# A four-layer graph network on one core: nodes without incoming edges put first, edge stages joined with the dense stages behind them

## The chip, the cores and the metric

The kernel runs on 1 core of a Trainium2 chip. Its time is the device time of one execution in microseconds, the median over several. A time without a unit is in microseconds. Engines: TensorE (PE; its weight loads are PEld), VectorE (DVE), ScalarE (ACT), GpSimd (POOL) and SyncE (SP, which only issues DMAs here).

## The reference

10000 nodes of 512 numbers and 5000 directed edges, sorted by target, go through four layers; each is followed by `x = layernorm(x + layer(x))`. Cut to what matters:

```
gin:  a = x + segment_sum(x[src], dst);  relu(a @ W1 + b1) @ W2 + b2
sage: m = segment_sum(x[src], dst) / max(count, 1)
      h = m @ W_l.T + b_l + x @ W_r.T;  relu(batch_norm(h)) + x
gat:  twice (edges and self loops, H = 4 heads of C = 256):
      h = (x @ W).reshape(n, H, C)
      e = leaky_relu(al_s[src] + al_d[dst], 0.2)        # al_s, al_d: h dotted with a_src, a_dst
      w = exp(e - segment_max(e, dst)[dst]);  alpha = w / segment_sum(w, dst)[dst]
      x = relu(segment_sum(h[src] * alpha, dst) + bias)
      then x @ Wfc + bfc
gcn:  dinv = (degree + 1) ** -0.5;  xw = x @ W.T
      h = segment_sum(dinv[row] * dinv[col] * xw[row], col) + b  # with self loops
      gelu(batch_norm(h)) + x
```

A node without an incoming edge has an empty sum: its GAT weight is 1 for itself and its GCN sum is its own row.

## The kernel before, in words

Nodes are padded to G = 20 groups of 512 (GROUP), each of S = 4 subtiles of 128 rows. Edges are T = 40 tiles of 128. The matrices are multiplied in half precision with a high and a low part: `split_product` (L316) issues three matmuls a chunk of 128 (L325, L326, L327).

The program is a list of stages (L2961). `run` (L278) gives every engine its part of a stage and then lets all five drain and meet on a semaphore, so a stage begins when the last engine is done with the one before. Inside a stage the order on an engine's queue is written out by hand. The stages are, with their place in the span: setup and the edge sum of the input; `gin_stage` (L1644); `edge_product_stage` (L1086); `sage_stage` (L1843); `norm_coefficients_stage`; `batch_norm_stage` (L2040, with the first GAT product, to `h1`); `edge_attention_stage` of `h1` (L1249); `gat_middle_stage` (L2298, to `h2`); `edge_attention_stage` of `h2`; `gat_stage` 2 (L2483, the last GAT product, to `x3`); `edge_sum_stage` of `x3` (L975); `gcn_stage` (L2738); the coefficients again; `output_stage` (L2858).

**Edge stages.** An edge stage goes over the 40 tiles. POOL gathers the source rows by an indirect DMA; a 128x128 matrix made from `apart` (which edges of the tile have different targets) sums rows with the same target on PE; SP stores the 128 sums of the tile to DRAM `sum` or `sum_gat` and, separately, its first and last row, for targets that cross from tile to tile (the rim, joined in a few steps at the end). In the attention stage a tile passes around a ring: ACT spreads the scores (L1496), PE turns them (L1543), DVE masks and takes maxima (L1380, L1385, L1387, L1391), ACT takes the exponential (L1511), PE sums the weights (L1552), DVE makes the matrix `a_lhs` of all four heads (L1397 to L1414), PE multiplies it with the gathered rows (L1560), ACT brings the result to SBUF (L1519), SP stores it. There are two buffers of `a_masked`, `a_lhs` and the score banks.

**Dense stages.** A node's sum lies in a slot that `slot_i` names, nodes without edges at a slot of zeros, so every dense stage starts with `gather_sums` (L1637): four indirect DMAs a group on POOL. In the GAT stages DVE combines own row and sums (`t_z`, L2415 and L2420, L2622), ACT applies bias and relu (L2433, L2656), makes the high part (L2436, L2659), POOL the low part (L2389, L2591). In GCN the low part is DVE's (L2798). In SAGE own rows come by one plain load a group, and PE turns both own rows (L1978) and sums. POOL adds the bias rows in GIN (L1732) and batch norm (L2161).

**Layer norm.** `Norm` (L1594): DVE takes statistics and aggregates (L1608, L1611), POOL raises variance to -1/2 (L1617, L1620), and a row operation applies it. The rows of the output stage: DVE adds residual and branch (L2923), `Norm`, POOL makes the shift `-mean * power` by two small operations (L2908, L2911), ACT applies (L2943), SP stores one group of 1 MB by one DMA (L2896):

```
sp.wait_ge(rows_out.sem, rows_out.at(g * S + S))
sp.dma_start(node_rows(dram["out"], *divmod(g, 2)), x[g])
```

## Time and profile before

| what | value |
| --- | --- |
| three runs | 3909.58, 3916.79, 3917.03; median 3916.79 |
| the profiled execution | 3912.85, its span 3911.1 |
| mean granted TensorE clock | 0.932 |
| busy PE / PEld / DVE / ACT / POOL | 3419.3 (87%) / 2074.1 (53%) / 2155.2 (55%) / 1463.1 (37%) / 1452.1 (37%) |
| DMA | 821.41 MB, mean 210 GB/s |

The stages, by the first and last instruction of each: setup and edge sum to 199.5; GIN to 659.5; edge product to 835; SAGE to 1131.5; coefficients to 1137; batch norm to 1627.5; attention of `h1` to 1812.7; GAT middle to 2687.9; attention of `h2` to 2873.5; second GAT product to 3402.1; edge sum of `x3` to 3495.6; GCN to 3758.5; coefficients to 3763.5; output to 3911.

A matmul's end is modelled, so a busy PE can still be slower than its peak. An engine's busy share over the whole span mixes stages with different limits, so the stages are read one by one.

### The profile page before, as it was taken

The page shows a single profiled execution, that of the slowest core. Times are in us where ns is not written, and L with a number is a line of the kernel's source. Part 1 is how long each engine was busy: PE and PEld are TensorE (multiplying, and loading weights), DVE is VectorE, ACT ScalarE, POOL GpSimd, SP SyncE. Part 2 cuts the span into 40 slices and gives each one's busy share as a digit, 9 for nine tenths or more (in the row PEclk, how much of TensorE's full clock was granted, in tenths as well). Part 3 has the DMA queues.
Part 4 walks back from the last instruction along what each step waited for, and adds up shares of the span by engine and source line. Part 5 has one row for each costly group of instructions (what it writes and reads, how often), then busy time and mean ns, then how long its engine had stood idle before and what let it go on. Part 6 is the DMA issues. An engine that isn't in the chain of part 4 may idle for free. (4 is left out here: it accounts for less than half of the span.)

```text
span 3911.1 us, 55988 instructions
## 1 busy us (share of the span) xinstructions
PE 3419.3 (87%) x19416; PEld 2074.1 (53%) x19416; DVE 2155.2 (55%) x3972; ACT 1463.1 (37%) x2580; POOL 1452.1 (37%) x1231
## 2 busy tenths in 40 slices
PE   4669998989969999886999999998859999859964
PEld 3234443545637666664666666666635555315543
DVE  7257775845554444276543443413758888406667
ACT  1323332533324444353332332322534444233357
POOL 2345553225422222253333323212536666343312
PEclk7789999989979999997999999999979999979976
DMA  2667774656659999597978878944957777375558
GB/s 82 201 184 198 196 201 146 201 172 228 227 195 259 279 274 281 180 280 213 256 192 204 204 194 198 200 119 146 280 209 259 262 261 262 123 231 186 174 167 275
DMA packets 624227, 821.41 MB, mean 210 GB/s; under 512 B 378374, under 2 KB 378374, under 8 KB 622032
## 3 DMA queue, kind: packets, MB, share of 16 engines
q1 hardware_dynamic: 556880, 598.37, 50.3%
q0 software_dynamic: 67200, 221.25, 20.1%
q8 instruction: 71, 1.16, 0.1%
q14 instruction: 76, 0.62, 0.1%
HBM read 470.83 MB, written 263.59 MB: 188 GB/s over the span
## 5 line engine op out<-in xcount | busy, mean ns | idle before, releaser
L326 PE MATMUL bank<-w_lo,t_r_hi 128*128 128x344 f16 (+1 forms) x2560 | 838.8, 328 | 0.0
L327 PE MATMUL bank<-w_hi,t_r_hi 128*128 128x344 f16 (+1 forms) x2560 | 838.6, 328 | 0.0
L325 PE MATMUL bank<-w_hi,w_lo 128*128 128x344 f16 (+1 forms) x2240 | 716.7, 320 | 49.8 <-DMA w_lo<-g_row_lo 31.3
L2415 DVE SCALAR_TENSOR_TENSOR t_z<-w_lo,t_z 128x256 f32<-128x256 f32 x320 | 243.5, 819 | 396.4 <-DMA w_lo<-h 393.4
L326 PE MATMUL bank<-w_lo,w_hi 128*128 128x344 f16 (+1 forms) x1280 | 419.6, 328 | 0.0
L327 PE MATMUL bank<-w_hi 128*128 128x344 f16 (+1 forms) x1280 | 419.4, 328 | 0.0
L2389 POOL TENSOR_TENSOR t_row_lo<-t_r,t_row_hi 128x1024 f16<-128x1024 f32 x80 | 174.9, 2187 | 509.8 <-ACT t_row_hi L2436 509.8
L327 PEld LDWEIGHTS bank<-w_hi,t_r_hi 128*128 128x128 f16 x2560 | 250.9, 98 | 168.8 <-issue 0.8
L326 PEld LDWEIGHTS bank<-w_lo,t_r_hi 128*128 128x128 f16 x2560 | 250.9, 98 | 162.5 <-issue 0.6
L325 PE MATMUL bank<-w_hi 128*128 128x344 f16 x960 | 298.3, 311 | 21.8 <-DMA w_hi<-t_row_lo 19.2
L325 PEld LDWEIGHTS bank<-w_hi,w_lo 128*128 128x128 f16 x2240 | 219.3, 98 | 181.7 <-issue 50.8
L325 PE MATMUL bank<-l_z_hi,w_lo 128*128 128x512 f16 x640 | 244.4, 382 | 1.4 <-DVE l_z_lo L2798 1.4
L326 PE MATMUL bank<-l_z_lo,w_hi 128*128 128x512 f16 x640 | 244.3, 382 | 0.0
L327 PE MATMUL bank<-l_z_hi,w_hi 128*128 128x512 f16 x640 | 244.1, 381 | 0.0
L325 PE MATMUL bank<-w_hi,t_r_lo 128*128 128x512 f16 x640 | 243.6, 381 | 0.0
L2591 POOL TENSOR_TENSOR t_r_lo<-t_r,t_r_hi 128x512 f16<-128x512 f32 x160 | 196.0, 1233 | 97.1 <-ACT t_r_hi L2659 90.1
L2447 ACT ACTIVATE w_hi<-bank 128x344 f32<-128x344 f32 x240 | 104.5, 454 | 339.5 <-PE bank L327 339.4
L2656 ACT ACTIVATE t_r<-bank,vec_scaled 128x512 f32<-128x512 f32 x160 | 109.6, 685 | 293.0 <-PE bank L2687 241.4
L1639 POOL DMA_INDIRECT t_z<-sum_gat,slot_i x160 | 163.0, 1019 | 122.0 <-SPq L292 79.1
L2243 ACT ACTIVATE b_wide<-bank 128x344 f32<-128x344 f32 x240 | 109.2, 456 | 253.1 <-PE bank L327 253.1
L1617 POOL TENSOR_TENSOR n_power<-n_moments,eps 128x4 f32<-128x4 f32 x80 | 15.9, 199 | 502.9 <-DVE n_moments L1611 502.9
L2622 DVE SCALAR_TENSOR_TENSOR t_z<-w_lo,t_z 128x256 f32<-128x256 f32 x320 | 187.0, 645 | 21.4 <-DMA t_z<-sum_gat,slot_i 13.3
(345 smaller groups left out, 6732.2 us busy)
## 6 DMA issues: line engine op xcount, KB each, us to landing
w_lo<-h SPq DMA_DIRECT2D x160, 512.0 KB, 5.7
h<-b_wide SPq DMA_DIRECT2D x80, 516.0 KB, 9.6
h<-w_hi SPq DMA_DIRECT2D x80, 516.0 KB, 2.9
sum_gat<-a_out SPq DMA_DIRECT2D x80, 514.0 KB
l_x<-x SPq DMA_DIRECT2D x40, 1024.0 KB, 9.1
sum<-e_out SPq DMA_DIRECT2D x120, 256.0 KB
g_x<-in_x SPq DMA_DIRECT2D x20, 1024.0 KB, 5.6
x<-g_y SPq DMA_DIRECT2D x20, 1024.0 KB, 5.1
```

Source lines behind the costliest of these rows:

```text
L325: pe.matmul(out, s_lo, m_hi, start=(k == 0), stop=False)
L326: pe.matmul(out, s_hi, m_lo, start=False, stop=False)
L327: mm = pe.matmul(out, s_hi, m_hi, start=False, stop=last)
L1617: self.nc.gpsimd.tensor_tensor(self.power[:, u, :], self.moments[:, u, :, 1], self.kn.eps[:], ALU.add)\
L1639: pool.indirect_dma_start(out, None, sums, bass.IndirectOffsetOnAxis(ap=kn.slot_i[:, g * S + s:g * S + s + 1], axis=0), bounds_check=kn.d. ...
L2243: act.activation(wide[s][:, n * THIRD:(n + 1) * THIRD], mm[n], ACT.Copy, scale=UNSCALE)\
L2389: nc.gpsimd.tensor_tensor(row_lo[:, s, :], r_f[s % 2][:], row_hi[:, s, :], ALU.subtract)\
L2415: ins = v.scalar_tensor_tensor(out=z[u][:, s, cols], in0=hrow[:, s, cols], scalar=z[u][:, s, HC + h:HC + h + 1], in1=z[u][:, s, cols], op0 ...
L2447: act.activation(wide[s % 2][:, third * THIRD:(third + 1) * THIRD], mm[s % 2][third], ACT.Copy, scale=UNSCALE).then_inc(wide_done.sem, 1)
L2591: g_.tensor_tensor(r_lo[:, u, k, :], r_f[k % 2][:], r_hi[:, u, k, :], ALU.subtract)\
L2622: ins = v.scalar_tensor_tensor(out=z[u][:, s, cols], in0=hrow[:, s, cols], scalar=z[u][:, s, HC + h:HC + h + 1], in1=z[u][:, s, cols], op0 ...
L2656: act.activation(r_f[k % 2][:], tp[k % 4][:], ACT.Relu, scale=A_SCALE, bias=kn.vec_scaled[:, bias + k:bias + k + 1]).then_inc(r_done.sem, 1)
```

## The change

After the change, "place" is a node's rank when nodes without an incoming edge come first. `d.early` = E = (10000 - 5000) // 1024 * 2 = 8 groups can't hold a node with an edge, whatever the graph.

- Setup ranks the nodes (a few operations on 128x80, three small matmuls), and keeps two tables in DRAM: `by_node` (dinv, place) and `by_place` (node, slot, dinv). GIN's POOL queue writes `by_place` by 80 small indirect stores, four behind the gathers of each group. The edge product stage reads it back, and POOL casts `slot_i` and `node_i`.
- GIN still works in node order. From SAGE on, rows lie by place: SAGE and batch norm fetch own rows of `x1` by four indirect DMAs a group on POOL (`own_rows`), where SP loaded a group at once. SAGE gathers, turns and adds sums for the last 12 groups alone. Batch norm's POOL queue also looks up place and dinv of all sources and targets (`look_up`, 80 in all, four a group).
- The two attention stages and the edge sum of `x3` are gone. The class `AttentionEdges` holds the same steps, each with one buffer of `a_masked`, `a_lhs` and scores, and the score turn as a transpose. `gat_middle_early_stage` and `rows_product_early_stage` run the first 8 groups, which need no sums, and carry 45 edge steps between their products: over 96 slots (three products a subtile) in the middle, over 32 in the second product. DVE makes the low parts in both, and `z * scale + bias` in the first; POOL only gathers for edges. `gcn_early_stage` does the same with `RowEdges`, 41 steps over 32 slots, on rows of `x3` that aren't scaled. `gat_middle_stage`, `gat_stage` and `gcn_stage` then go over 12 groups, written as before.
- The output rows lie by place: SP's plain store becomes four indirect stores a group on POOL, queued behind the next group's `Norm` and shift. DVE makes `-mean` (one operation on 128x4 a group), POOL has one small operation less.
- Small tables per edge lie in one SBUF buffer.

```diff
+        self.early = max(nodes - edges, 0) // (2 * GROUP) * 2
...
+def own_rows(kn, pool, out, g, s, landed):
+    pool.indirect_dma_start(out, None, kn.dram["x1"],
+                            bass.IndirectOffsetOnAxis(ap=kn.node_i[:, g * S + s:g * S + s + 1], axis=0),
+                            bounds_check=kn.d.padded - 1, oob_is_err=False).then_inc(landed.sem, 16)
...
+def shared_out(steps, slots):
+    return [range(n * steps // slots, (n + 1) * steps // slots) for n in range(slots)]
...
+class AttentionEdges:
+    W, O = 4, 3
...
+    def matrices(self, dve, t):
+        dve.wait_ge(self.den_done.sem, self.den_done.at(t + 1))
+        v.tensor_tensor(self.out[o][:, A_DEN], self.den_ps, self.weight[u][:, 0, :], ALU.add).then_inc(self.den_kept.sem, 1)
+        if t + 2 < self.T:
+            self.scores(dve, t + 2)
...
+        dve.wait_ge(self.summed.sem, self.summed.at(t))
+        v.scalar_tensor_tensor(out=self.lhs[:], in0=self.kn.apart[:, t, :].unsqueeze(1).broadcast_to([P, K, P]),
+                               scalar=0.0, in1=self.out[o][:, A_EDGE].unsqueeze(2).broadcast_to([P, K, P]),
+                               op0=ALU.is_equal, op1=ALU.mult).then_inc(self.lhs_ready.sem, 1)
...
+    def vector(self, dve, t):
+        self.matrices(dve, t)
+        if t + 1 < self.T:
+            self.maxima(dve, t + 1)
...
+    def steps(self):
+        return self.T + 5
...
+    def tensor(self, pe, t):
+        w = t % self.W
+        pe.wait_ge(self.lhs_ready.sem, self.lhs_ready.at(t + 1))
+        pe.wait_ge(self.evacuated.sem, self.evacuated.at(2 * t))
+        for h in range(HEADS):
+            ins = pe.matmul(self.total[h // 2][:, (h % 2) * C:(h % 2 + 1) * C], self.lhs[:, h, :],
+                            self.rows[w][:, LOGITS + h * C:LOGITS + (h + 1) * C], start=True, stop=True)
+        ins.then_inc(self.summed.sem, 1)
+        if t + 1 < self.T:
+            self.sum_weights(pe, t + 1)
+        if t + 2 < self.T:
+            self.score_rows(pe, t + 2)
...
+def gat_middle_early_stage(kn):
...
+    steps = shared_out(edges.steps(), THIRDS * N)
...
+        for j in range(N):
+            for third in range(THIRDS):
+                if j + S < N and third == 0:
+                    add_bias(j + S)
+                if j + S < N and third == 2:
+                    low_part(j + S)
+                for e in steps[j * THIRDS + third]:
+                    edges.vector_step(dve, e)
...
+            for third in range(THIRDS):
+                pe.wait_ge(wide_done.sem, wide_done.at((j - 1) * THIRDS + third + 1))
+                split_product(pe, mm[third],
+                              lambda k: (r_hi[u][:, s * CH + k, :], r_lo[u][:, s * CH + k, :]),
+                              lambda k: (kn.gat_weights(False, W_GAT2, k, third),
+                                         kn.gat_weights(True, W_GAT2, k, third)), CH).then_inc(prod.sem, 1)
+                for e in steps[j * THIRDS + third]:
+                    edges.tensor_step(pe, e)
...
+def rows_product_early_stage(kn):
...
+    steps = shared_out(edges.steps(), E * S)
...
+        low_parts(0, range(CH))
+        edges.vector_start(dve)
+        for g in range(E):
+            for s in range(S):
+                if g + 1 < E:
+                    low_parts(g + 1, (2 * s, 2 * s + 1))
+                residual(g, s)
+                for e in steps[g * S + s]:
+                    edges.vector_step(dve, e)
+                if s == 1 and g:
+                    finish(g - 1)
+        finish(E - 1)
...
+            for s in range(S):
+                if g + 1 < E:
+                    turn(g + 1, (2 * s, 2 * s + 1))
+                pe.wait_ge(y_done.sem, y_done.at(g * S + s - 1))
+                split_product(pe, mm[s % 2][:],
...
+def gcn_early_stage(kn, held):
...
+    edges = RowEdges(kn, room, dram["x3"], (kn.src_by[:, :, 0], kn.src_dinv_neg), kn.dst_dinv, kn.rim_dinv)
+    steps = shared_out(edges.steps(), 4 * E)
...
 def output_stage
-            sp.dma_start(node_rows(dram["out"], *divmod(g, 2)), x[g])\
-                .then_inc((first_stored if g < B else stored).sem, 16)
...
+        def store(g):
+            pool.wait_ge(rows_out.sem, rows_out.at(g * S + S))
+            for s in range(S):
+                pool.indirect_dma_start(dram["out"],
+                                        bass.IndirectOffsetOnAxis(ap=kn.node_i[:, g * S + s:g * S + s + 1], axis=0),
+                                        x[g][:, s, :], None, bounds_check=d.padded - 1, oob_is_err=False)\
+                    .then_inc((first_stored if g < B else stored).sem, 16)
...
-            nc.gpsimd.tensor_tensor(shift[:, u, :], norm.moments[:, u, :, 0], norm.power[:, u, :], ALU.mult)\
-                .then_inc(shifted.sem, 1)
-            pool.wait_ge(shifted.sem, shifted.at(g * 2 + 1))
-            nc.gpsimd.tensor_scalar(shift[:, u, :], shift[:, u, :], -1.0, None, ALU.mult).then_inc(shifted.sem, 1)
+            pool.wait_ge(negated.sem, negated.at(g + 1))
+            nc.gpsimd.tensor_tensor(shift[:, u, :], shift[:, u, :], norm.power[:, u, :], ALU.mult).then_inc(shifted.sem, 1)
+            if g:
+                store(g - 1)
...
+            dve.wait_ge(norm.seen.sem, norm.seen.at((g + 1) * 2 * S))
+            v.tensor_scalar(shift[:, u, :], norm.moments[:, u, :, 0], -1.0, None, ALU.mult).then_inc(negated.sem, 1)
...
-        kn.add(edge_attention_stage(kn, dram["h1"]))
+        kn.add(gat_middle_early_stage(kn))
         kn.add(gat_middle_stage(kn))
-        kn.add(edge_attention_stage(kn, dram["h2"]))
+        kn.add(rows_product_early_stage(kn))
         kn.add(gat_stage(kn, 2))
...
-            kn.add(edge_sum_stage(kn, mem, dram["x3"], (kn.src_dinv, kn.src_dinv_neg), kn.dst_dinv, kn.rim_dinv))
...
+            kn.add(gcn_early_stage(kn, held))
             kn.add(gcn_stage(kn, held))
```

## Rows read from the trace of the kernel before

**Rows 1.** Busy time by stage; us, busy (x instructions) by engine, PEclk, DMA, GB/s.

```profile
1627.50:1812.70 185.20, 143.87 (x748) 111.26 (x748) 122.94 (x462) 84.12 (x201) 79.79 (x80) 0.92 0.77 232
1812.70:2687.90 875.20, 847.35 (x5776) 567.60 (x5776) 343.81 (x402) 259.93 (x401) 254.92 (x160) 0.98 0.79 193
2687.90:2873.50 185.60, 143.40 (x748) 111.02 (x748) 122.97 (x462) 84.01 (x201) 79.66 (x80) 0.92 0.77 232
2873.50:3402.10 528.60, 489.73 (x2560) 262.61 (x2560) 388.05 (x640) 202.87 (x320) 303.52 (x280) 0.96 0.65 239
3402.10:3495.60 93.50, 54.16 (x82) 16.85 (x82) 1.16 (x2) 42.51 (x80) 39.99 (x40) 0.79 0.72 227
3495.60:3758.50 262.90, 245.92 (x1280) 131.25 (x1280) 154.07 (x240) 94.38 (x160) 81.38 (x80) 0.96 0.52 160
3763.50:3911.00 147.50, 67.88 (x320) 60.88 (x320) 117.33 (x241) 115.08 (x160) 33.25 (x80) 0.59 0.85 285
```

**Rows 2.** The same view, in the middle of five dense stages.

```profile
2000.00:2435.00 435.00, 435.00 (x2985) 291.73 (x2983) 183.02 (x210) 132.68 (x206) 132.86 (x85) 1.00 0.83 198
3000.00:3250.00 250.00, 250.00 (x1318) 133.35 (x1317) 202.22 (x332) 102.12 (x162) 157.23 (x146) 1.00 0.72 263
1290.00:1534.00 244.00, 244.00 (x1720) 170.31 (x1718) 113.34 (x219) 111.16 (x217) 58.51 (x32) 1.00 0.94 279
3560.00:3691.00 131.00, 131.00 (x696) 70.17 (x695) 83.01 (x130) 50.62 (x87) 43.97 (x43) 1.00 0.57 177
900.00:1048.50 148.50, 148.50 (x860) 89.23 (x859) 84.64 (x129) 50.03 (x87) 71.77 (x72) 1.00 0.66 224
```

**Rows 3.** Timeline of an attention tile; start, us, engine, what, idle before and releaser.

```profile
1700.26 2.00 PE L1560 MATMUL bank<-a_rows,a_lhs 128*128 128x256 f32 x8 [0.42 <-DVE a_lhs L1414]
1702.29 0.39 PE L1552 MATMUL bank<-a_weight,a_same 128*128 128x4 f32 x2
...
1703.35 0.69 DVE L1414 SCALAR_TENSOR_TENSOR a_lhs<-apart,a_out 128x512 f32<-128x512 f16 x1
...
1704.09 2.00 PE L1560 MATMUL bank<-a_rows,a_lhs 128*128 128x256 f32 x8 [0.43 <-DVE a_lhs L1414]
```

**Rows 4.** Timeline near the end of the output stage, and the chain's last row.

```profile
3893.57 0.69 DVE L1608 BATCH_NORM_STATS2 n_stats<-o_x 128x6 f32<-128x512 f32 x1
3894.41 0.18 DVE L1611 BATCH_NORM_AGGREGATE n_moments<-n_stats 128x2 f32<-128x6 f32 x1
...
3895.02 1.04 POOL L1620 TENSOR_TENSOR n_power<-n_power,minus_half 128x4 f32<-128x4 f32 x1
...
3901.61 1.04 POOL L1620 TENSOR_TENSOR n_power<-n_power,minus_half 128x4 f32<-128x4 f32 x1
...
3904.79 1.41 ACT o_x L2943 x2
```

**Rows 5.** PE's timeline: transposes in the second product, products of the edge sum.

```profile
3360.61 1.04 PE L2687 MATMUL bank<-ident,t_z 128*128 128x128 f32 x8
...
3482.18 2.05 PE L1076 MATMUL bank<-e_rows,e_lhs 128*128 128x512 f32 x4 [1.35 <-ACT e_out L1065]
```

**Rows 6.** Timeline: first product of two stages, last residual of the second.

```profile
1837.02 0.47 PE L325 MATMUL bank<-w_hi 128*128 128x344 f16 x1 [19.19 <-DMA w_hi<-t_row_lo]
...
2911.49 0.63 PE L325 MATMUL bank<-w_hi,t_r_lo 128*128 128x512 f16 x1
...
3392.77 0.69 DVE L2639 SCALAR_TENSOR_TENSOR w_hi<-bank,w_hi 128x512 f32<-128x512 f32 x1 [3.43 <-PE bank L327]
```

**Rows 7.** POOL: gathers in GIN, in GCN; bias in batch norm; landing in SAGE.

```profile
L1639 POOL DMA_INDIRECT g_z<-sum,slot_i x43 | 62.6, 1455 | 11.9 <-issue 11.9
...
L1639 POOL DMA_INDIRECT l_z<-sum,slot_i x43 | 44.0, 1023 | 81.0 <-PE bank L2838 70.9 <-issue 10.1
...
1398.48 4.51 POOL L2161 TENSOR_TENSOR b_o<-b_o,fc_b 128x2048 f32<-128x2048 f32 x1 [7.40 <-DVE b_row_lo L2197]
...
l_a<-sum,slot_i POOLq DMA_INDIRECT x44, 4.2
```

More of the change, by code:

```diff
@@ L806, in tensor @@
             ins.then_inc(looked_up.sem, 1)
+        pe.wait_ge(alone_steps.sig.sem, alone_steps.sig.at(3))
+        pe.wait_ge(table_ready.sem, table_ready.at(B))
+        pe.matmul(alone_total_ps, alone[:], kn.ones[:], start=True, stop=True).then_inc(products.sem, 1)
         pe.wait_ge(ties_ready.sem, ties_ready.at(B))
@@ L812, in tensor @@
         ins.then_inc(products.sem, 1)
+        pe.wait_ge(ranked.sem, ranked.at(1))
+        pe.matmul(ranks_ps[:, 0:K], above, alone[:], start=True, stop=False)
+        pe.matmul(ranks_ps[:, 0:K], alone_total[0:K, :], above[0:K, 0:K], start=False, stop=True)
+        pe.matmul(ranks_ps[:, K:K + 1], alone_total[0:K, :], kn.ones[0:K, 0:1], start=True, stop=True)\
+            .then_inc(products.sem, 1)
         pe.wait_ge(table_ready.sem, table_ready.at(B))
@@ L1668, in gin_stage @@
     x_in = pair("x_in", 16 * H)
-    sum_in = pair("sum_in", 16 * S * H, software=True)
+    sum_in = [take(f"sum_in{u}_0", 16 * S * H, software=True) for u in range(2)]
     z_ready = pair("z_ready", H * S)
@@ L1744, in gpsimd @@
                 load_sums(g + 3)
+            for k in range(g * S, g * S + S):
+                store_by_place(k)
+        pool.wait_ge(table_out.sem, table_out.at(16 * d.blocks))
     def vector(dve):
@@ L2162, in bias, with load_own @@
                 .then_inc(biased[u].sem, 1)
-        def group(i, u, last):
-            norm.pool(pool, i, u)
-            bias(i, u)
-        if sage:
-            in_pairs(pool, G, group)
-        else:
-            in_pairs(pool, G, lambda i, u, last: norm.pool(pool, i, u))
+        def load_own(g):
+            i, u = divmod(g, 2)
+            pool.wait_ge(y_done[u].sem, y_done[u].at(i * S))
+            for s in range(S):
+                own_rows(kn, pool, x[u][:, s, :], g, s, x_in[u])
+        sides = [(kn.src_by, kn.src_at_i), (kn.dst_by, kn.dst_at_i)]
+        ends = [(out, at, t) for t in range(d.tiles) for out, at in sides]
+        per = -(-len(ends) // G)
+        load_own(0)
+        load_own(1)
+        for g in range(G):
+            norm.pool(pool, *divmod(g, 2))
+            if g + 2 < G:
+                load_own(g + 2)
+            bias(*divmod(g, 2))
+            for out, at, t in ends[g * per:(g + 1) * per]:
+                look_up(kn, pool, out, at, t, found)
+        pool.wait_ge(found.sem, found.at(16 * 2 * d.tiles))
+        nc.gpsimd.tensor_copy(kn.src_i[:], kn.src_by[:, :, 1]).then_inc(negated.sem, 1)
+        nc.gpsimd.tensor_scalar(kn.dst_logits_i[:], kn.dst_by[:, :, 1], float(GAT_ROW // LOGITS), None, ALU.mult)\
+            .then_inc(negated.sem, 1)
+        pool.wait_ge(negated.sem, negated.at(2))
+        nc.gpsimd.tensor_scalar(kn.src_dinv_neg[:], kn.src_by[:, :, 0], -1.0, None, ALU.mult).then_inc(negated.sem, 1)
+        pool.wait_ge(negated.sem, negated.at(3))
     def vector(dve):
@@ L2767, in sync @@
     def sync(sp):
-        for g in range(G):
+        for g in range(N):
             i, u = divmod(g, 2)
@@ L2821, in scalar @@
         high_parts(0)
-        for g in range(G):
+        for g in range(N):
             for m in range(4):
-                if g + 1 < G and m == 1:
+                if g + 1 < N and m == 1:
                     high_parts(g + 1)
-                own = held.rows[g][m]
+                own = held.rows[E + g][m]
                 act.wait_ge(mid.sem, mid.at(g * 4 + m + 1))
@@ L2841, in tensor @@
         turn(0)
-        for g in range(G):
+        for g in range(N):
             u = g % 2
```

1405 lines of the change are left out of this document (977 added, 428 removed).

## The prediction, made before the change was timed

> **What bounds the kernel now.** I read first the busy times by stage [rows 1], the stages told apart by the first and last instruction of each. Three stages treat edges alone: two attention stages of 185.2 and 185.6 us and an edge sum of 93.5 us. The reader is to see that none of the three keeps an engine full (in the attention stage PE 144, DVE 123, ACT 84, POOL 80 of 185 us), while the dense stages behind them run at a full TensorE: their middles [rows 2] show PE busy without a gap (435.00 of 435.00 us) at granted clock 1.00. Dividing those windows by their matmul records gives the period of a group of 512 nodes: GAT middle 435/2985 x 288 = 42.0 us; second GAT product 250/1318 x 128 = 24.3; GCN 131/696 x 64 = 12.05; SAGE 148.5/860 x 80 = 13.8; batch norm with the first GAT product 244/1720 x 160 = 22.7. Times 20 groups (41.97, 24.28 and 12.05 unrounded) and taken from the stage [rows 1], that leaves 35.8 us of start and end around the GAT middle, 43 around the second product and 22 around GCN.
>
> Third, the timeline of one attention tile [rows 3]: from one `a_lhs` product to the next 3.83 us. It is a ring, not a full engine: DVE makes the maxima, ACT the weights, PE the sum of weights, DVE the matrix, PE the product. Last, the output stage, where DVE's records follow one another without a gap, a group takes 6.6 us from one `n_power` to the next [rows 4], and PE is busy for less than half [rows 1].
>
> The change moves the 40 edge tiles of each edge stage onto the queues of the first 8 groups of the next dense stage, which have no edges to wait for. So the question is what a tile costs on PE's path, and what the renumbering costs on POOL.
>
> **GAT middle with attention.** PE's share of a tile [rows 3]: products 2.00, the sum of weights 0.39; the score turn becomes a transpose, 8 of which take 1.04 us [rows 5], so 4 take 0.44 by their spacing. Less the overlap of the ends some 2.75 us. Bounds for a tile: 2.75 (all else hidden) and 3.83 (the whole ring, nothing hidden). I take 2.75 here, because 45 edge steps lie in 96 slots, one in two of 3.5 us, so each ring has about 7 us to close; DVE in that stage has 123/40 = 3.1 us of edge work a tile [rows 1] and gains some 2.4 us a subtile (add_bias and the low part, in place of 4 combines and a bias add), far below PE. Late stage: 875.2 - 8 x 42.0 = 539.2. Early: 8 x 42.0 + 35.8 + 40 x 2.75 = 481.8; the start, 24 us until the first product [rows 6], stays about as long, since DVE must do eight operations on 1024 columns and the first ring before PE starts, where it had to wait for gathered sums. With 2 us for the rim steps: 1023 against 185.2 + 875.2 = 1060.4, so **-37**.
>
> **Second product with attention.** Here 45 steps lie in 32 slots, so 13 slots hold two. In such a slot PE ends its product at T, and the second step needs the ring: DVE first does its residual and the statistics behind it (0.69 [rows 6] and as much again, about 1.9 us with the small ones), then the weights are turned into a matrix (1.36 us from the end of the weights' product to the end of `a_lhs` [rows 3]), then makes the maxima (two passes as long as `a_lhs`, 0.69 us, and two small ones), and ACT the weight. I get T + 6.8 us instead of T + 5.5, with a little for semaphores 1.6 us a slot, 21 in all (bounds 0 and 13 x 3.83 = 50). The start gets shorter: the first product came 38 us after the stage began [rows 6], behind gathers and combines; now plain rows are loaded, eight parts made on ACT, and one ring closed, about 28 us; bounds 20 and 38. DVE's low parts (8 a group; I put them at the 0.69 us of `a_lhs`, which has as many columns) and 15 us of edge work make about 30 us a group beside 38 us of PE, so they cost nothing while PE stays the longer. Early: 8 x 24.3 + 110 + 21 + 28 + 10 (the tail in rows 6, residual to store) = 363.4. Late: 528.6 - 8 x 24.3 = 334.2. Sum 697.6 against 714.2: **-17**.
>
> **GCN with the edge sum.** PE pays 2.05/2 = 1.0 us a tile at most [rows 5], 39 in all; what paced the edge sum at 93.5/40 = 2.3 us a tile [rows 1] (SP's DMAs, PE being busy for 54 of 93.5 us) has some 3 us or more between two steps. Start 15 (no sums, no scaling), where start and end together are 22 now, and tail 10 for the rim (DMA, product, two DVE operations, store). Early 96.4 + 39 + 15 + 10 = 160.4; late 262.9 - 96.4 = 166.5; sum 326.9 against 93.5 + 262.9: **-29.5**.
>
> **SAGE.** Eight groups lose 16 transposes and an add: the period falls from 13.8 to GCN's 12.05, -14. The rows now come by four gathers a group behind POOL instead of one plain load; the first turn waits for four gathers 1.30 us apart (in GCN 1.02 and 0.3 of issue) [rows 7] and their landing, where it waited for one load: +3. In late groups POOL issues 8 gathers, 10.4 us of 13.8, and the own rows of the next group are queued behind the sums: the last is issued after 9.1 us and lands 4.2 after that [rows 7], 13.3, just inside the period. **-11**, bounds -14 and +2.
>
> **POOL elsewhere.** Batch norm: 4 gathers and 4 look-ups a group, 10.4 us, beside 4.5 us of bias [rows 7] and 1.3 us of powers (as in rows 4), 16.2 of 22.7 us; `bias` stands behind gathers that fill a wait of 7.4 us which POOL has there. I take +2, bounds 0 and +20. GIN: 4 small scatters a group behind its gathers, which already stretch to 1.75 us there [rows 7], so 7 us more in groups of over 20; POOL then comes later to `add_bias`, whose result is needed a group later: 0, and +1 for the last landing; bounds 0 and +20 (1 us a group). Setup: a few small operations, and PE waits once for ACT's copy; +1. The edge-product stage gains one load and two casts under its last tiles: 0.
>
> **Output.** Once per group DVE gets a 128x4 `tensor_scalar` that waits for the last aggregate; a wait and an operation of that size take 0.15 + 0.18 = 0.33 us [rows 4], 20 times, +6.6 on the chain that ends last. The plain 1 MB store from SP becomes four indirect stores on POOL. Their price isn't in this trace; the nearest rows are the gathers, 1.30 us apart where nothing disturbs them and 1455 + 300 ns = 1.75 us in GIN [rows 7]. At 1.30 POOL has 5.2 + 1.65 (1.04 of powers [rows 4] and three small operations) = 6.85 us a group beside DVE's 6.6 + 0.33: a tie, +1 to 3. At the end the store of group 18 stands in front: POOL is free for group 19 about 2 us after ACT is done and needs 5.2 us for the four, where one DMA now ends the span at 3911.1, 4.9 us after ACT's last row [rows 4]: +5. **+14**, bounds +8 and (at 1.75) +46.
>
> **Sum:** 1 + 1 - 11 + 2 - 37 - 17 - 29.5 + 14 = -76.5. The profiled execution took 3912.85 us around a span of 3911.1; 3836.4. The median of the three runs is 3.9 us above it: **3840 us**. About 0.2% (8 us) is what a measurement of this kernel can tell from no change.
>
> **A rule against it.** Of 43 gathers each, those of GIN take 1455 ns and those of GCN 1023 [rows 7]. The difference goes with what DVE does: in GIN it runs operations with two operands in SBUF (`add_sums`, both low parts), in GCN the second operand of most lies in PSUM. [...]
>
> **Rivals.** (1) *The ring isn't hidden.* All 80 attention tiles cost 3.83: +43 in the middle, +43 - 21 in the product: 3905 us. For it: in-order queues, one `masked`, one `lhs`, one bank of scores where there were two. Against: the slots computed above. Chance 0.14. (2) *POOL paces moderately*, 1.75 us per indirect DMA everywhere: output 8.65 us a group, +46 in place of +14; SAGE's late groups 14.0 us instead of 13.8, +2; batch norm 19.8, still hidden: 3874 us, chance 0.13. (3) *POOL paces, and the kernel gets slower.* One mechanism: POOL's interval x of one indirect DMA in the stages that gained them. Beyond the terms above, output costs 20 x (4x + 1.65 - 6.6), SAGE 12 x (8x - 13.8), batch norm 20 x (8x + 5.8 - 22.7). At 2.0 us these eat the gain; at 2.4 they come to 98, 65 and 46 us, and the time is 3840 + 84 + 65 + 44, near 4030. For it: GIN's mean of 1.75 [rows 7], stores to DRAM of this kind are new, and DMA is busy 0.85 of the output stage [rows 1]. Against: in GCN 1.30 holds, and DVE works there as it does in the output. Chance 0.07. That the change doesn't do what it says I exclude: 10000 nodes less 5000 edges fix 8 early groups whatever the graph.
>
> **Numbers.** Forecast 0.62 with its own range 3800 to 3865; 0.14, 0.13 and 0.07 for the rivals; 0.04 for gains and losses that cancel. Low end: no loss in double slots (-21), output +8, SAGE -14, some 10 us of starts: 3793. High end takes in rivals 1 and 2, not their sum. Faster 0.88, same 0.04, slower 0.08.
>
> **What would show it.** Right: joined middle near 480 us with PE above 0.95 busy; joined product near 363 with PE waiting 1 to 2 us for `a_lhs` or `a_weight` in 13 slots; joined GCN near 160; SAGE some 11 us shorter; output near 161, POOL's indirect stores 1.0 us each. Wrong: a granted clock below 1.00 inside the joined stages, PE idle before most `a_lhs` products, POOL without waits in output or SAGE, or starts of the joined stages over 40 us.

## The result and the profile after

| | before | changed | with three edits (last experiment) |
| --- | --- | --- | --- |
| median | 3913.18 (n = 4) | 3815.35 (n = 4) | 3792.88 (n = 5) |
| ratio to before, 95% interval | 1 | 0.9748 [0.9728, 0.9768] | 0.9686 [0.9669, 0.9703] |
| span of the profiled execution | 3911.1 | 3812.3 | 3796.2 |

The change made the kernel 98 us faster; 76.5 had been worked out. One run of the changed kernel was a slow one (4938.06 us, clock 0.69); it is in the median of four and left out of the ratio. The before of the last column was measured again beside it (3913.89, n = 9).

The busy time by stage of the changed kernel (us, busy time and instructions of PE, PEld, DVE, ACT, POOL, granted clock, DMA share, GB/s), in the order GIN, SAGE, batch norm, joined and late GAT middle, joined and late second product, joined and late GCN, output:

```profile
200.60:666.60 466.00, 419.96 (x1920) 186.64 (x1920) 316.82 (x560) 149.54 (x240) 309.81 (x220) 0.95 0.71 181
841.40:1128.90 287.50, 268.85 (x1472) 154.65 (x1472) 135.66 (x209) 94.56 (x160) 135.26 (x131) 0.96 0.59 191
1133.60:1625.60 492.00, 462.39 (x3200) 320.25 (x3200) 207.15 (x400) 205.49 (x400) 291.42 (x223) 0.97 0.85 257
1625.60:2081.60 456.00, 436.69 (x2892) 315.84 (x2892) 198.07 (x528) 155.65 (x330) 83.79 (x80) 0.98 0.79 206
2081.60:2616.50 534.90, 510.67 (x3472) 342.60 (x3472) 203.71 (x242) 156.63 (x241) 155.40 (x96) 0.97 0.76 189
2616.50:2987.20 370.70, 316.69 (x1604) 203.37 (x1604) 226.63 (x654) 161.67 (x329) 92.10 (x96) 0.91 0.65 207
2987.20:3321.60 334.40, 295.19 (x1536) 159.21 (x1536) 231.16 (x384) 121.64 (x193) 182.93 (x168) 0.94 0.62 226
3321.60:3473.30 151.70, 137.54 (x594) 69.87 (x594) 45.48 (x66) 80.00 (x144) 39.99 (x40) 0.93 0.61 196
3473.30:3640.50 167.20, 149.53 (x768) 79.68 (x768) 92.64 (x145) 56.84 (x97) 48.35 (x48) 0.93 0.53 151
3645.00:3812.30 167.30, 68.46 (x320) 61.29 (x320) 120.89 (x260) 115.06 (x160) 108.38 (x140) 0.60 0.74 251
```

Set against the stages of before (attention and edge sum counted with the dense stage behind them), that gives this account. The last column is the term of the prediction. The two short stages of coefficients (10.5 us before, 9.2 after) are left out.

| stages | before | after | moved by | forecast |
| --- | --- | --- | --- | --- |
| setup | 199.5 | 200.6 | +1 | +1 |
| GIN | 460.0 | 466.0 | +6 | +1 |
| edge product | 175.5 | 174.8 | -1 | 0 |
| SAGE | 296.5 | 287.5 | -9 | -11 |
| batch norm | 490.5 | 492.0 | +1.5 | +2 |
| attention and GAT middle | 1060.4 | 990.9 | -69.5 | -37 |
| attention and second product | 714.2 | 705.1 | -9 | -17 |
| edge sum and GCN | 356.4 | 318.9 | -37.5 | -29.5 |
| output | 147.5 | 167.3 | +20 | +14 |

A single profile doesn't fix such a stage to the microsecond. In the other profiles of this study in which a stage was left as it is, SAGE took 290.0 to 293.6 us (eleven profiles; 287.5 above is the shortest), the joined second product 361.4 to 374.4 (five profiles) and the late GAT middle 534.7 to 544.9. GIN took 464.7 to 466.7 and the setup 199.8 to 203.3, so the setup's +1 is 0 to +4. Output (166.9 to 167.3), batch norm (491.9 to 492.2) and the joined middle (456.0 to 458.3) repeat within 2 us. I read a difference in the first three as real only where it leaves these ranges. In the joined second product most of the scatter goes with the granted clock: 374.4 us at 0.90 and 361.4 at 0.94, with PE's waits for `a_lhs` at 22.5 to 25.5 us in all six profiles.

**The middle, where most came from.** PE's timeline of the joined stage, one edge tile between two products (start, us, what):

```profile
1803.72 0.31 PE L352 MATMUL bank<-w_hi,t_r_hi 128*128 128x344 f16 x1
1803.86 1.89 PE L1700 MATMUL bank<-a_rows,a_lhs 128*128 128x256 f32 x8
1805.59 0.28 PE L1687 MATMUL bank<-a_weight,a_same 128*128 128x4 f32 x2
1805.73 0.63 PE L1679 MATMUL bank<-ident,a_spread 128*128 128x128 f32 x4
1806.20 0.31 PE L350 MATMUL bank<-w_hi 128*128 128x344 f16 x1
```

No row has an idle time before it. Counted from start to start, the tile costs PE 1806.20 - 1803.86 = 2.34 us, of a ring that took 3.83 by itself [rows 3]. It holds for all tiles: from one tile's product to the next PE takes 9.34 us, two products of 3.5 and one tile, in 33 of 39 cases, and 12.84, with a third product between, in five.

**The second product.** Its -9 is between the -5 and -18 that the six profiles of the joined stage (361.4 to 374.4) would give, so the shortfall against -17 isn't shown; the waits are. PE's and DVE's waits there between 2650 and 2970 (what waits, for what, us, times, longest), and a piece of the timeline at the start of a group:

```profile
DVE w_hi L3043 <- DMA w_hi<-x_biased: 33.1, 6, 7.7
...
PE bank L1700 <- DVE a_lhs L1521: 25.5, 11, 6.3
...
DVE a_score L1471 <- DMA a_rows<-h,edge_tables: 20.0, 10, 4.7
```

```profile
2778.05 0.69 DVE L3043 SCALAR_TENSOR_TENSOR w_hi<-bank,w_hi 128x512 f32<-128x512 f32 x1 [7.67 <-DMA w_hi<-x_biased]
...
2780.31 0.69 DVE L1521 SCALAR_TENSOR_TENSOR a_lhs<-apart,a_out 128x512 f32<-128x512 f16 x1
...
2781.06 3.35 PE L1700 MATMUL bank<-a_rows,a_lhs 128*128 128x256 f32 x7 [6.27 <-DVE a_lhs L1521]
```

The reader is to see a chain of three: the rows for the residual land 7.67 us late, DVE takes the residual first and makes `a_lhs` 2.3 us later, and PE stands 6.27 us for it. The load is `load_x(g)`, which SP issues in slot 1 of the very group whose slot 0 needs it. Of PE's 11 waits for `a_lhs`, five are of this kind (2.26 to 6.27 us, 19.6 together): in each, DVE had been idle for at most 0.25 us since it stood for late residual rows. The other six are the double slots with nothing late, 0.90 to 1.23 us, 5.9 together. One of them:

```profile
2670.03 0.64 PE L1679 MATMUL bank<-ident,a_spread 128*128 128x128 f32 x4
2671.60 1.99 PE L1700 MATMUL bank<-a_rows,a_lhs 128*128 128x256 f32 x8 [0.94 <-DVE a_lhs L1521]
```

The long wait cost more than itself. The same view of busy times as above, for a slot before it and for the product behind it:

```profile
2763.90:2772.20 8.30, 8.30 (x47) 5.35 (x46) 5.81 (x16) 4.40 (x9) 3.65 (x4) 1.00 1.04 363
...
2781.06:2784.60 3.54, 3.54 (x10) 2.89 (x11) 1.55 (x4) 0.21 (x1) 0.00 (x0) 0.54 0.05 16
```

The granted clock was 1.00, TensorE idled for 6.27 us, and the product behind it ran at 0.54, close to the lower level of 1.2 GHz: 3.35 us for its first seven matmuls, where eight took 1.89 above. Over the stage the clock was 0.91, in the joined middle 0.98.

**The output.** POOL's last rows, from the chain that ended last and from the timeline, and the stretch behind them in the view of busy times:

```profile
3784.30 1.04 POOL n_power L1859
...
3791.35 1.04 POOL n_power L1859
...
3794.22 1.42 ACT o_x L3716 x2
```

```profile
3800.94 0.97 POOL L3665 DMA_INDIRECT out<-o_x,place_at_i  x1 [0.30 <-issue]
3802.21 0.97 POOL L3665 DMA_INDIRECT out<-o_x,place_at_i  x1 [0.30 <-issue]
```

```profile
3805.00:3812.30 7.30, 0.00 (x0) 0.00 (x0) 0.00 (x0) 0.00 (x0) 0.00 (x0) 0.50 0.00 0
```

A group takes 3791.35 - 3784.30 = 7.05 us on POOL, which has no wait of its own there, where it was 6.6 on DVE [rows 4]. ACT's last row ends at 3795.64, POOL's last store is out at 3803.18, and the span ends 9.1 us later; in its last 7.3 us the DMA engines move nothing at all.

### The profile page after: what moved, and what is told of

Read it like the earlier page. It is cut to its first block and busy times, and to the rows that moved or that the text cites. A ratio compares the mean times of both kernels' runs of the same rounds, so it can differ in the third digit from the quotient of the medians.

```text
span 3812.3 us, 54507 instructions
## 1 busy us (share of the span) xinstructions
PE 3331.3 (87%) x18968; PEld 2030.1 (53%) x18968; DVE 2002.7 (53%) x3782; ACT 1427.9 (37%) x2551; POOL 1561.8 (41%) x1355
## 5 line engine op out<-in xcount | busy, mean ns | idle before, releaser
L352 PE MATMUL bank<-w_hi 128*128 128x344 f16 (+1 forms) x1280 | 420.5, 329 | 0.0
L350 PE MATMUL bank<-w_hi 128*128 128x344 f16 (+1 forms) x1216 | 397.0, 326 | 19.7 <-DMA w_hi<-t_row_lo 19.7
L1438 POOL DMA_INDIRECT a_own<-h,edge_tables x80 | 82.1, 1026 | 611.7 <-PE bank L1700 433.0
L2875 DVE SCALAR_TENSOR_TENSOR t_z<-w_lo,t_z 128x256 f32<-128x256 f32 x192 | 144.5, 811 | 196.7 <-DMA w_lo<-h 193.7
L2849 POOL TENSOR_TENSOR t_row_lo<-t_r,t_row_hi 128x1024 f16<-128x1024 f32 x48 | 106.0, 2210 | 277.5 <-ACT t_row_hi L2896 277.4
L1700 PE MATMUL bank<-a_rows,a_lhs 128*128 128x256 f32 x640 | 158.6, 392 | 25.5 <-DVE a_lhs L1521 25.5
L352 PEld LDWEIGHTS bank<-w_hi 128*128 128x128 f16 x1280 | 126.0, 98 | 85.3 <-issue 0.8
L351 PEld LDWEIGHTS bank<-w_lo,w_hi 128*128 128x128 f16 x1280 | 126.0, 98 | 84.3 <-issue 0.8
L350 PEld LDWEIGHTS bank<-w_hi 128*128 128x128 f16 x1216 | 119.9, 99 | 93.2 <-issue 21.3
L1878 POOL DMA_INDIRECT t_z<-sum_gat,slot_i x96 | 100.2, 1043 | 117.1 <-SPq L317 91.4
L1700 PEld LDWEIGHTS bank<-a_rows,a_lhs 128*128 128x128 f32 x640 | 122.3, 196 | 48.3 <-DVE a_lhs L1521 29.0
```

The source lines that it names most:

```text
L350: pe.matmul(out, s_lo, m_hi, start=(k == 0), stop=False)
L351: pe.matmul(out, s_hi, m_lo, start=False, stop=False)
L352: mm = pe.matmul(out, s_hi, m_hi, start=False, stop=last)
L1438: pool.indirect_dma_start(self.own[w][:], None, self.logits_dram, bass.IndirectOffsetOnAxis(ap=kn.dst_logits_i[:, t:t + 1], axis=0), bound ...
L1700: ins = pe.matmul(self.total[h // 2][:, (h % 2) * C:(h % 2 + 1) * C], self.lhs[:, h, :], self.rows[w][:, LOGITS + h * C:LOGITS + (h + 1) * ...
L1878: pool.indirect_dma_start(out, None, sums, bass.IndirectOffsetOnAxis(ap=kn.slot_i[:, g * S + s:g * S + s + 1], axis=0), bounds_check=kn.d. ...
```

## The experiments

Twelve variants of the changed kernel. "Joined product" is `rows_product_early_stage`, "joined middle" is `gat_middle_early_stage`. Since the stages are parted by a barrier, each run is read by the length of the stage that it edits. All but the last ran once, so a difference inside the scatter of a stage says nothing.

### The ring made longer

```diff
-        v.scalar_tensor_tensor(out=self.lhs[:], ...).then_inc(self.lhs_ready.sem, 1)
+        for done in (self.lhs_once, self.lhs_ready):
+            v.scalar_tensor_tensor(out=self.lhs[:], ...).then_inc(done.sem, 1)
+            dve.wait_ge(done.sem, done.at(t + 1))
```

> In both joined attention stages DVE makes the matrix a_lhs of every tile twice, the second after the first (some 0.85 us more per tile on DVE and in the ring). Theory, the ring is hidden and PE sets the pace: in the joined GAT middle (456.0 us in the changed kernel, no wait of PE for a_lhs) nothing changes, at most 2 us; in the joined second product (370.7 us, PE waits 25.5 us for a_lhs in 11 waits) only the slots with two edge steps pay, 11 to 13 times 0.85, so about 381. Rival, the ring of a tile is what a tile costs: both stages grow by 40 x 0.85 = 34 us.

Joined middle 456.0, as before; joined product 383.0 (361 to 374 unedited), with 31.8 us of PE's waits for `a_lhs` in place of 25.5. In the middle the added work on the ring, 34 us by my estimate, vanishes: it is hidden there, and PE sets the pace. In the product a part of it comes through: 383.0 is 9 us above the longest time of the stage unedited.

### One edge step in every slot

```diff
-    steps = shared_out(edges.steps(), THIRDS * N)
+    steps = shared_out(edges.steps(), 48) + [range(0)] * (THIRDS * N - 48)
```

> In the joined GAT middle the 45 edge steps lie in the first 48 of the 96 slots, one in every slot but three, where they lay in every second. Theory A, a slot of 3.5 us with 2.34 us of edge work on PE still hides the ring of 3.83 us: the stage stays at 456, within 3 us. Rival B, spacing is what hides it: DVE, the gathers or SP's stores of a tile are late each time, PE waits for a_lhs, 0.5 to 1.5 us a tile, and the stage takes 475 to 515 us. (DMA is busy for 0.79 of this stage; the edges' share then falls on half the time.)

The joined middle took 514.3 us: +58, rival B. The waits between 1645 and 1880 of PE (the 12.0 is the start's, as in the changed kernel) and of DVE, and the view of busy times over most of the dense steps:

```profile
PE bank L1679 <- ACT a_spread L1627: 12.0, 1, 12.0
PE bank L1687 <- issue: 11.4, 4, 3.4
PE bank L1700 <- DVE a_lhs L1521: 10.7, 5, 3.9
PE bank L1687 <- ACT a_weight L1642: 10.7, 5, 4.8
```

```profile
DVE a_out L1509 <- PE bank L1687: 45.9, 27, 7.2
DVE a_score L1471 <- DMA a_rows<-h,edge_tables: 43.4, 13, 6.4
DVE a_out L1493 <- DMA a_last<-a_out: 23.4, 8, 4.8
```

```profile
1650.00:1850.00 200.00, 171.66 (x1021) 126.04 (x1022) 97.26 (x305) 71.74 (x163) 51.44 (x50) 0.93 0.90 215
```

My expectation A was wrong. A slot of 5.84 us is longer than the ring, and the ring closes in it: in 16 of 39 cases PE goes from one tile's product to the next in exactly 5.84 us, without a wait. In the others it takes up to 13.2. What is late then is transfers, as far as the waits tell: DVE stands 43.4 us for gathered rows (4.3 in the same window of the changed kernel) and 23.4 us until SP has stored an output buffer (0.6), with the DMA engines busy for 0.90 of the time. Of the 58 us, 21 are a longer busy time of PE (457.8 against 436.7) at a granted clock of 0.94 in place of 0.98. So the spacing of one step in two slots is what hides the tiles in the middle, and it hides the transfers more than the ring. No run with fewer transfers in the same slots was made.

### The residual rows loaded earlier, and the residual behind the edge steps

Joined product, two edits, each alone and then together:

```diff
-                if s == 1 and g >= 2:
+                if s == 0 and g >= 2:
                     load_x(g)
```

> In the joined second product SP issues the load of a group's residual rows one slot earlier (slot 0 in place of slot 1 of the group that needs it). Theory A, the late load is what makes a good part of PE's 25.5 us of waits for a_lhs: DVE stood 33.1 us in 6 waits for those rows, in front of the matrix. The DVE waits fall below 10 us, PE's to 12 to 16, the stage from 370.7 to 357 to 361. Rival B, the double slots alone cause PE's waits through the order on DVE: DVE's waits go and the stage stays within 3 us of 370.7.

```diff
-                residual(g, s)
                 for e in steps[g * S + s]:
                     edges.vector_step(dve, e)
+                residual(g, s)
```

> In the joined second product DVE takes the edge steps of a slot before the residual of that slot, where the residual came first. Theory A, what stands ahead of a_lhs on DVE's queue (1.9 us of residual and statistics, and its wait for late rows) makes PE's 25.5 us of waits: they fall below 8 us and the stage from 370.6 to 350 to 354. Rival B, another link of the ring is late as well (the gathers of the tile after next stand in the same step: 20.0 us of DVE waits in the changed kernel): PE's waits stay above 10 us and the stage at 356 or more. Rival C, the residual now comes too late for PE's next bank: new waits of PE for y, the stage no shorter.

> The joined second product with both edits: residual rows loaded one slot earlier, and DVE's residual behind the edge steps of its slot. Theory A, once the residual stands behind the steps, the late load holds up nothing but the residual, so the load adds little: the stage takes 345 to 350 us (349.2 with the order alone). Rival B, the two gains add (14 and 21 us): 335 to 338.

Loaded earlier: 356.5 us, and DVE's wait for the rows is gone from its list. Residual last: 349.2. Both: 354.3. PE's waits for `a_lhs` in the three, in this order:

```profile
PE bank L1700 <- DVE a_lhs L1521: 16.4, 13, 2.7
```

```profile
PE bank L1700 <- DVE a_lhs L1521: 12.7, 10, 2.7
```

```profile
PE bank L1700 <- DVE a_lhs L1521: 16.9, 13, 2.9
```

So theory A of the first holds (the late load was a part, below the 361 to 374 of the stage unedited), and in the second A holds for the stage and B for the waits: they don't fall below 8. Together they aren't better than the order alone, as expected, since what stands behind the edge steps can be late without harm. 354.3 against 349.2 is inside the scatter of this stage and tells nothing.

The third run says more when it is set beside the first. With the load early, the order changes neither PE's waits (16.4 us with the residual first, 16.9 with it last) nor, beyond the scatter, the stage (356.5 and 354.3). So the order helps by keeping late rows from standing ahead of the matrix. The 1.9 us of residual and statistics cost PE nothing that is seen here: the commonest wait of a double slot is 0.94 us in the changed kernel and in all three runs. The longest in the three runs, 1.7 to 2.9 us, come where DVE stands for gathered rows.

### Half slots

This stands on both edits before it.

```diff
+    halves = shared_out(edges.steps(), 2 * E * S)
+    steps = [list(halves[2 * n]) + list(halves[2 * n + 1]) for n in range(E * S)]
...
+                if k == CH // 2:
+                    for e in halves[2 * (g * S + s)]:
+                        edges.tensor_step(pe, e)
```

> As the run before it, and the 45 edge steps lie in 64 half slots (a step can also stand in the middle of a product, after four of its eight chunks), so no two follow one another without products of 2.6 us or more between them. Theory A, what is left of PE's waits for a_lhs (12.7 us in 10) comes from two steps back to back: they fall below 3 us and the stage to 334 to 340. Rival B, the gathers set it (38 us of DVE waits for rows of the tile after next, four buffers deep): steps closer together elsewhere keep the waits, the stage stays within 3 us of the run before.

349.4 us, 4.9 less than with both orders and the same as with the residual last alone. That is far from the 334 to 340 of theory A and nearer to rival B, whose 3 us it leaves only by the scatter of the stage. PE's and DVE's waits:

```profile
PE bank L1687 <- ACT a_weight L1642: 6.7, 2, 4.6
PE bank L1700 <- DVE a_lhs L1521: 5.6, 6, 3.1
```

```profile
DVE a_score L1471 <- DMA a_rows<-h,edge_tables: 39.5, 17, 8.2
```

The wait for `a_lhs` falls from 16.9 to 5.6, and another for the weights takes its place. What stays in every variant is DVE's wait for gathered rows: 37.8, 38.3, 40.9 and 39.5 us in the four, against 20.0 in the changed kernel. They stand in the middle of the matrix of a tile, because `matrices(t)` makes the raw scores of tile t + 2 before the reciprocal. That this wait is what bounds the stage now is argued from these rows and not shown; no run with more gather buffers was made.

### The low parts on POOL

The eight subtractions of 128x512 a group moved from DVE's queue to POOL's, ahead of POOL's norm and gathers in each slot.

> In the joined second product POOL makes the low parts (eight subtractions of 128x512 a group), where DVE makes them in the changed kernel. Theory A, they lie beside the product before the residual on DVE and cost nothing there: the stage stays at 370.6, within 3 us. Rival B, they stand before a_lhs and cost in the slots with two steps: 8 to 15 us shorter on POOL. Rival C, POOL's queue waits for free gather buffers ahead of them, so PE waits for low parts: 10 us longer or more.

365.4 us, inside the 361 to 374 of the stage unedited; PE's waits for `a_lhs` 24.5 us in 11. Theory A: that DVE makes the low parts costs nothing that can be seen in the joined product. On DVE one took 684 ns in the changed kernel, the 0.69 of the prediction.

### GIN's table stores earlier

```diff
-            for k in range(g * S, g * S + S):
+            for k in range(g * (S + 1), min((g + 1) * (S + 1), d.blocks)):
```

> GIN's POOL queue issues five small table stores a group over the first 16 groups in place of four over all 20. Theory A, GIN's 5.6 us are the last four stores, issued after the last norm and 6 us from being done: the stage falls from 466.0 to 460 to 461. Rival B, the stores lengthen POOL's turn, so that add_bias comes late: with five a group the stage is as long as before or 1 us a group longer, 466 to 480.

GIN took 460.3 us: theory A. The rows of the changed kernel at the end of GIN show the same: the last small store is out at 660.73, and the next stage's first row comes 6 us later.

```profile
659.75 0.98 POOL L1989 DMA_INDIRECT by_place<-place_table,place_at_i  x1 [0.30 <-issue]
...
666.77 0.98 ACT L1270 ACTIVATE e_lhs<-apart,ones 128x128 f32<-128x128 f16 x3 [24.07 <-POOLq L317]
```

### The output stored plainly, and POOL's queue made shorter

In the first, SP stores a group by one DMA of 1 MB, as before the change, and the rows stay in the order by place. In the second, beside a store of group 18 put ahead of the last power:

```diff
-            norm.pool(pool, i, u)
-            nc.gpsimd.tensor_tensor(shift[:, u, :], shift[:, u, :], norm.power[:, u, :], ALU.mult)
+            nc.gpsimd.tensor_tensor(norm.power[:, u, :], both[:, u, :, 1], minus_half, ALU.pow)
+            nc.gpsimd.tensor_tensor(shift[:, u, :], both[:, u, :, 0], norm.power[:, u, :], ALU.mult)
...
-            v.tensor_scalar(shift[:, u, :], norm.moments[:, u, :, 0], -1.0, None, ALU.mult)
+            v.scalar_tensor_tensor(out=both[:, u, :, :], in0=norm.moments[:, u, :, :], scalar=EPS, in1=sign[:],
+                                   op0=ALU.add, op1=ALU.mult)
```

> The output rows are stored by SP, 1 MB a group, as before the change; DVE's small operation stays. Putting the rows back into the order of the nodes is left out. Theory A, POOL's queue paces the output at 7.05 us a group and eight stores with a long landing stand behind ACT's last row: the stage falls from 167.3 to about 154 (6.9 us a group, 4.9 us behind ACT's last row), the kernel to about 3802. Rival B, the stage's 20 us come from DVE's operation on 128x4 with its wait: it falls by less than 5 us.

> Output stage: DVE's small operation makes minus mean and variance plus eps at once (128x8; minus mean is off by the eps of 1e-5), POOL has one operation less, waits for each row tile instead of a group, and stores group 18 before it raises the last variances. Theory A, POOL's queue sets the stage: the turn of a group falls from 7.05 to DVE's 6.93 us, and behind ACT's last row 16.7 become about 14: the stage falls from 167.3 to 160 to 162. Rival B, the writes to rows in DRAM themselves or their landing set the pace: the stage stays within 2 us of 167.3.

Plain: 150.8 us, 16.5 less, a bit more than A said. ACT's last rows end at 3797.24 and the span 4.8 us behind them:

```profile
3795.74 1.50 ACT L3708 ACTIVATE o_x<-o_x,o_shift,n_power 128x512 f32<-128x512 f32 x2
3797.26 0.37 SPq L3661 DMA_DIRECT2D out<-o_x  x1
```

So of the stage's 20 us some 3.3 are the edits that stayed, DVE's operation among them (150.8 against 147.5; a group takes 6.79 us in this run), and the rest is POOL: 16.7 - 4.8 = 12 behind ACT's last row, and the turn of 7.05 us. Shorter queue: 163.7, 3.6 less where 5 to 7 were expected. The turn fell by more than expected, to 6.78 us. Part of the reason is my order for the last group. The stores of group 18 were put ahead of the power of group 19, which then came late:

```profile
3794.92 0.97 POOL L3668 DMA_INDIRECT out<-o_x,place_at_i  x1 [0.31 <-issue]
3795.91 1.05 POOL L3682 TENSOR_TENSOR n_power<-o_both,minus_half 128x4 f32<-128x4 f32 x1
...
3802.79 0.98 POOL L3668 DMA_INDIRECT out<-o_x,place_at_i  x1 [0.30 <-issue]
```

ACT waited 8.94 us for the last shift, where it was 4.12. With the old order (the last experiment) the stage took 162.8, only 0.9 less, so the order isn't all of it. The end is again 9.3 us behind the last store (3803.77 to 3813.1), so the length of POOL's queue ahead of it doesn't set that time.

### SAGE with plain loads

Own rows by one load of 1 MB a group on SP, no `own_rows` on POOL; the order of the rows by place is left out.

> SAGE loads its own rows by one plain load a group on SP, as before the change, where POOL gathers four times a group; that the rows then stand in the order of the nodes (the permutation) is left out. Theory A, as the forecast had it: the gathers cost only the first turn, 3 us, and the stage takes 284 to 289 (287.5 to 293.6 in the runs so far; 13.8 us of 12.05 + turns a group are PE's). Rival B, POOL's eight gathers a late group hold up the sums: the stage falls to 280 or less, and its spread from run to run goes.

SAGE took 281.6 us, where the twelve profiles with gathers lie at 287.5 to 293.6 (the changed kernel's own included). That falls between A and B, nearer to B: the gathers cost 6 to 12 us, not 3. Of these 2.8 are the first wait (11.6 us for gathered rows against 8.8). For the rest no cause is shown: behind that first wait PE doesn't wait for gathered rows in the changed kernel's profile.

### Three edits together

Residual last, GIN's stores five a group, and the shorter POOL queue with the changed kernel's order of groups kept.

> Three edits on the changed kernel: in the joined second product DVE takes the residual behind the edge steps (349 against 361 to 374 us in six looks at that stage unchanged), GIN's table stores five a group over 16 groups (460.3 against 466), and the output's POOL queue one operation shorter with a wait for each row tile, group order as in the changed kernel (minus mean off by 1e-5). If the stages are independent of each other, as the barrier between them says: 3812 - 20 - 6 - 4 = 3782 to 3788 in the profiled execution, a ratio to the kernel before of 0.967 (0.965 to 0.969). Rival, what one stage gives up returns as later transfers in the next: 3795 or more, 0.970 or above.

Ratio 0.9686 [0.9669, 0.9703], median 3792.88: faster than the changed kernel, whose interval begins at 0.9728. The ratio is the one expected. The edited stages gave what they had given alone: GIN 460.3, joined product 350.8, output 162.8. The profiled execution (3798.03, the longest of the five, 3791.65 to 3798.03) is above the 3782 to 3788 expected, and above the 3795 at which I had put the rival. I had subtracted from a profile with a short SAGE, 287.5; here it took 293.4, and the late middle 538.6, both inside their ranges. The stages behind the edited ones are no longer than in the other profiles (edge product 175.8, late second product 334.3), so nothing is seen to return there.

## Why the prediction was right, and where it was off

The forecast held: faster, 3840 with a range of 3790 to 3900, measured 3815. The mechanism was the one described: edge stages that kept no engine full moved beneath dense stages that PE paces, less a price on POOL's side. That the total is within 25 us owes something to luck: middle and GCN brought 40 us more than their terms, and GIN, SAGE, second product and output 21 us less. In the second product the mechanism was wrong although the number fits. Point by point:

- **GAT middle (-37, measured -69.5).** Two terms mis-sized in the same direction. A tile was put at 2.75 us on PE from the durations of its groups of matmuls; from start to start it is 2.34, 16 us over 40 tiles, and below the 2.75 that was given as the lower bound. In the rows above the three durations, 1.89, 0.28 and 0.63, sum to 2.80; each runs on beside the start of the next. And start and end were kept at 35.8 us "about as long": the first product came 19.3 us after the stage began (1644.95), not 24, and start and end took 456 - 336 - 94 = 26 us. The late stage took 535 where 539 was worked out. PE was busy for 0.96 of the joined stage, as forecast. That the ring is hidden was right, which the first experiment shows; but the reason given (about 7 us for each ring) asks for the wrong thing. The ring closed in 5.84 us too; what that spacing no longer hid was, by DVE's waits, the transfers.
- **Second product (-17, measured -9).** Start 28 predicted, 28.2 measured (2616.5 to 2644.67). Stalls 21 predicted, 25.5 measured, and that they agree is luck. The prediction had 1.6 us in each of 13 double slots, because residual and statistics stand ahead of the matrix. A double slot with nothing late costs 0.94 us, whichever stands first. 19.6 of the 25.5 us are five waits behind a late load of residual rows, seen in the diff and not followed through SP's queue. Turning the order round took the stage to 349.2 and 350.8 us (361 to 374 unedited) because it moves that load out of the way. What was left out too is the clock: 0.91 over the stage and 3.35 us for seven matmuls behind a wait.
- **GCN (-29.5, measured -37.5).** A tile cost 0.86 us between the start of its product (3338.16) and the next row (3339.02), not 1.0, and the first product came 12.3 us after the start, not 15. The two make 8 of the 9 us by which the joined stage stayed below its 160.4:

```profile
3338.16 1.02 PE L1827 MATMUL bank<-w_lo 128*128 128x512 f32 x2
3339.02 0.60 PE L3478 MATMUL bank<-ident,l_x 128*128 128x128 f32 x4
```

- **SAGE (-11, measured -9, in other profiles -3 to -7).** The eight lighter groups gave 15 us (the run with plain loads), as computed; the gathers cost 6 to 12 in place of 3. Whether that is the 13.3 us of "just inside the period" of 13.8 is not shown; the cause beyond the first wait stays open.
- **GIN (+1, measured +6).** The turn of POOL didn't matter, as argued; the end did. The term "+1 for the last landing" was 6 us.
- **Output (+14, measured +20).** The tie of DVE (6.93 us a group) and POOL (6.85) was no tie: a group takes 6.79 in the run with plain stores, so DVE's operation costs some 0.2 and not 0.33, and POOL sets the pace at 7.05. And 9.1 us of landing stood where 4.9 was taken over from a plain store.

No rival came: the ring is hidden in the middle, and POOL's indirect stores took 0.99 us and 0.3 of issue. But two of the signs of being wrong did: POOL without waits in the output, which cost 20 us in place of 14 and not the 46 of rival 2, and a clock below 1.00 in the joined stages, 0.98 in the middle and 0.91 in the product. The low end of the sum was added up wrongly: 3840 less 21, 6, 3 and 10 is 3800, not 3793. Nothing hangs on it.

Of GIN's long gathers, which rival 2 took for every indirect DMA, the trace shows this much. POOL's gathers by stage, GIN, SAGE, batch norm and joined product, and its stores in the output:

```profile
L1878 POOL DMA_INDIRECT g_z<-sum,slot_i x80 | 110.3, 1378 | 43.7 <-issue 22.0 <-SPq L317 21.6
...
L1885 POOL DMA_INDIRECT l_x<-x,place_at_i x80 | 79.8, 997 | 114.4 <-PE bank L2238 54.3 <-SPq L317 38.1 <-issue 21.9
...
L1885 POOL DMA_INDIRECT b_x<-x,place_at_i x80 | 95.2, 1190 | 24.4 <-issue 23.0 <-DVEq L317 1.4
...
L1438 POOL DMA_INDIRECT a_own<-h,edge_tables x36 | 36.9, 1025 | 207.8 <-PE bank L1700 174.1 <-DVE a_score L1472 26.7 <-issue 7.0
...
L3665 POOL DMA_INDIRECT out<-o_x,place_at_i x30 | 29.8, 992 | 10.8 <-issue 10.2 <-DVE n_moments L1850 0.3 <-ACT o_x L3716 0.3
```

They take 1378 ns in GIN and 1190 in batch norm. In the joined product they don't stretch (1025 against 997 in SAGE), though DVE makes low parts from two SBUF operands there for 35 of 320 us. By the section "SBUF: two separate sides" of the page SBUF — State Buffer of the Trainium skill, a DVE operation with two SBUF inputs and a GpSimd operation shut each other out only where the latter reads SBUF. Whether that is what stretches these gathers no run here shows, and none shows that the stretch moved the time of a stage.

## What to carry to other kernels

When work is laid into the slots of a paced engine, count its price from start to start of that engine's rows at full clock, and give the slots the transfers' pace too: one step in two slots cost 2.34 us each, one in every slot 58 us more in all. Ahead of the critical step on an in-order queue put nothing that can wait for a transfer: moving the residual behind the edge steps took a stage from 361 to 374 us to 349 to 351. And price an indirect DMA at the end of a stage by its landing, not by its issue.

## What the hardware showed that I had not expected

The end of an indirect store is long: 9.0 to 9.6 us from the end of POOL's last instruction to the end of the span in the twelve profiles with such stores, and 6.0 us for 12-byte rows in GIN, against 4.8 us from ACT's last row to the end with a plain 1 MB store. During the last 7.3 us of the changed kernel no DMA engine moved data; what fills that time no run shows. And the length of one stage with many gathers and stores differs by up to 13 us between profiles of the same code (361.4 to 374.4 us, at granted clocks of 0.94 and 0.90), while the whole kernel differed by 5 us in three executions (3811.56 to 3816.50).
